# Keys laid out by halves, a result left transposed, and engine orders written group by group

## What is computed

```python
def _cma(x1, x2, ln1_g, ln1_b, ln2_g, ln2_b, Wq, bq, Wk, bk, Wv, bv, Wo, bo):
    x1n, x2n = _ln(x1, ln1_g, ln1_b), _ln(x2, ln2_g, ln2_b)
    q, k, v = x1n @ Wq + bq, x2n @ Wk + bk, x2n @ Wv + bv
    attn = softmax(einsum('bqe,bke->bqk', q, k) * E ** -0.5)
    return einsum('bqk,bke->bqe', attn, v) @ Wo + bo
res = _cma(x, c, ...) + _cma(x, f, ...) + x
x1 = _ln(res, ln_g, ln_b) @ fc_W + fc_b + res
Q, K, V = x1 @ Wq + bq, c @ Wk + bk, c @ Wv + bv
out = x1 + softmax(Q K^T * 128 ** -0.5) V @ Wo + bo
```

## Time and profile before

| what | value |
| --- | --- |
| median of 3 runs | 215.62 us (215.46 to 215.97) |
| the profiled execution | 217.09 us, span 215.3 us |
| mean granted TensorE clock | 0.96 |
| PE busy | 184.8 us (86%) |
| DVE busy | 168.8 us (78%) |
| POOL busy | 148.7 us (69%) |
| ACT busy | 141.8 us (66%) |
| DMA | 22.16 MB, mean 103 GB/s |

### The profile page before, as it was taken

The page is one execution under the profiler, slowest core; times in us unless marked ns, Lnnn a source line. Parts: engine busy times, 40 slices in busy tenths (PEclk is TensorE's granted clock), DMA queues, the critical chain, the costliest instruction groups (busy, mean ns, idle before and its releaser), DMA issues.

```text
span 215.3 us, 6455 instructions
## 1 busy us (share of the span) xinstructions
PE 184.8 (86%) x2380; PEld 138.8 (64%) x2380; DVE 168.8 (78%) x613; ACT 141.8 (66%) x381; POOL 148.7 (69%) x267
## 2 busy tenths in 40 slices
PE   0499687989899999999999999999999999896942
PEld 0386466767676767677776767777676767564531
DVE  5573675888989898989898989899999696966212
ACT  2336681777778787878787877878786866465140
POOL 1878878889797979787878787888788860412000
PEclk9999996999999999999999999999999999998585
DMA  5630441322325151616160807080704050204011
GB/s 148 190 146 2 148 142 59 100 97 95 106 79 169 51 195 30 218 32 218 9 237 6 240 5 232 15 242 9 238 13 146 3 146 3 97 3 146 0 50 52
DMA packets 13570, 22.16 MB, mean 103 GB/s; under 512 B 1825, under 2 KB 4129, under 8 KB 13538
## 3 DMA queue, kind: packets, MB, share of 16 engines
q1 hardware_dynamic: 13538, 21.74, 31.9%
HBM read 17.54 MB, written 4.19 MB: 101 GB/s over the span
## 4 chain that ended last, share of the span: by engine, by line
DVE 44%; PE 29%; ACT 11%; issue 11%; DMA 2%; SPq 1%; DVEq 0%
ACT exp L459 10%; PE ps_s L833 8%; DVE s_m L637 7%; DVE stats L634 6%; DVE out_sb L585 6%; DVE max L620 5%; DVE res_sb L630 5%; DVE sum L570 5%; PE ps_d L734 4%; PE ps_g L819 3%; DVE minus_max L592 2%; DVE rsum L572 2%; DVE s_diff L641 2%; DMA w_sb<-in_w 2%; PE ps_g L745 1%
## 5 line engine op out<-in xcount | busy, mean ns | idle before, releaser
L354 POOL TENSOR_TENSOR rstd<-st_var,minus_half 128x4 f32<-128x4 f32 (+1 forms) x32 | 42.6, 1332 | 2.2
L485 ACT ACTIVATE z_sb<-x_sb,shift,rstd 128x128 f32<-128x128 f32 x64 | 26.4, 485 | 6.8 <-POOL shift L362 6.8
L383 POOL TENSOR_TENSOR resb_sb<-res_sb,row_bias 128x512 f32<-128x512 f32 x16 | 20.4, 1275 | 13.8 <-DVE res_sb L630 13.7
L585 DVE SCALAR_TENSOR_TENSOR out_sb<-ps_g,rsum,x_sb 128x128 f32<-128x128 f32 x64 | 17.9, 343 | 7.7 <-PE ps_g L745 7.7
L387 POOL TENSOR_TENSOR rstd<-s_var,minus_half 128x4 f32<-128x4 f32 x16 | 16.3, 1017 | 10.1 <-DVE s_var L645 10.1
L620 DVE TENSOR_REDUCE max<-ps_s 128x8 f32<-128x512 f32 x16 | 11.1, 692 | 14.0 <-PE ps_s L833 14.0
L459 ACT ACTIVATE exp<-ps_s,minus_max 128x64 f32<-128x64 f32 x64 | 19.2, 312 | 3.5 <-DVE minus_max L592 2.6
L604 DVE SCALAR_TENSOR_TENSOR x_sb<-ps_d,rstd,resb_sb 128x128 f32<-128x128 f32 x64 | 17.9, 342 | 4.4 <-PE ps_d L803 4.4
L516 DVE BATCH_NORM_STATS2 stats<-cf_sb 128x6 f32<-128x64 f32 x128 | 18.7, 212 | 2.1 <-DMA cf_sb<-in_cf 2.1
L494 ACT ACTIVATE t_sb<-ps_d,t_bias 65x512 f32<-65x512 f32 x16 | 10.9, 683 | 12.1 <-PE ps_d L752 12.1
L778 PE MATMUL ps_z<-zT_sb,m 128*128 128x512 f32 x32 | 18.1, 649 | 0.8 <-ACT zT_sb L436 0.8
(11 more groups left out here) (141 smaller groups left out, 460.3 us busy)
## 6 DMA issues: line engine op xcount, KB each, us to landing
cf_sb<-in_cf SPq DMA_DIRECT2D x16, 256.0 KB, 2.6
x_sb<-in_x SPq DMA_DIRECT2D x16, 256.0 KB, 3.0
xres_sb<-in_x SPq DMA_DIRECT2D x16, 256.0 KB, 4.5
out<-out_sb SPq DMA_DIRECT2D x16, 256.0 KB, 4.2
ct_sb<-in_ct SPq DMA_DIRECT2D x16, 128.0 KB, 4.6
c_sb<-in_c SPq DMA_DIRECT2D x16, 128.0 KB, 4.3
w_sb<-in_w SPq DMA_DIRECT2D x1, 384.0 KB
w_score_sb<-in_w_score SPq DMA_DIRECT2D x1, 128.0 KB, 2.3
```

The costliest lines, as they stand in the source:

```text
L354: pool.tensor_tensor(rstd0[:, slot, cols], st_var[:, cols], minus_half[:, cols], ALU.pow).then_inc(st_rstd_done, 1)
L383: pool.tensor_tensor(resb_sb[:, :, :], res_sb[:, slot, :, :], row_bias[:, :].unsqueeze(1).broadcast_to([P, PAIRS, D]), ALU.add).then_inc(r ...
L485: last = nc.scalar.activation(z_sb[:, slot, p, :], x_sb[:, slot, p, :], ACT.Identity, bias=shift0[:, slot, p:p + 1], scale=rstd0[:, slot, ...
L585: last = v.scalar_tensor_tensor(out_sb[:, slot, p, :], ps_g[:, p % 2, (p // 2) * D:(p // 2 + 1) * D], rsum1[:, p:p + 1], x1_sb[:, slot, p, ...
```

## The change

- Keys by halves. cf is laid out in memory by_keys: the partition halves now hold two sequences' keys (v) with c and f side by side, so that c1 is not loaded at all and mix1 reads cf_sb. s0's output has the query's sequence on the partition halves and the source in two banks. s0 and mix1 go through the four corners of the array in the order TILES = (0,0), (1,1), (1,0), (0,1).
- Result transposed. out1 has w1 as its weights and makes the result transposed; the final step is one addition with x1T, and the host transposes. The second softmax is therefore scaled by rsum1 ahead of its transpose (probs1); exp1 is written back into ps_r. row_bias becomes a column that the x1T copy adds, and resb is gone.
- x and cf have a buffer for each group and are loaded once; most intermediates have two buffers or more.
- The banks: ps_s (two) serves cfT, s0, prob1T and mix1; ps_r serves resT and s1.
- The variance of res moves to GpSimd for groups 4 to 12; the power of the statistics is one operation. For groups 0 and 1 VectorE takes the variance and ScalarE normalises cf (early_cfn); ScalarE copies the first folds and issues the first weight loads.
- The step loop is gone: each engine has a list of calls with their groups written out. Each TensorE call also waits until its bank has been read (bank_read).

The diff, cut to its core:

```diff
-LAG_STATS, LAG_NORM, LAG_SCORE, LAG_MIX, LAG_DENSE, LAG_ATT1, LAG_FINAL, LAG_STORE = range(8)
-STEPS = GROUPS + LAG_FINAL
-SLOTS = 2
...
+EARLY = 2
+AHEAD = 4
+X_SLOTS, CT_SLOTS, OUT_SLOTS = GROUPS, 5, 3
+CFN_SLOTS, RES_SLOTS, X1T_SLOTS, RSTD_SLOTS, Z_SLOTS, SLOTS = 4, 4, 4, 4, 3, 2
+VAR1_ON_POOL = range(4, 13)
...
@@ PSUM banks @@
-        ps_z = bank("ps_z", [P, 512])
-        ps_s0 = bank("ps_s0", [P, 512])
-        ps_s1 = bank("ps_s1", [P, 512])
-        ps_d = bank("ps_d", [P, 512])
-        ps_o0 = bank("ps_o0", [P, 512])
-        ps_g = bank("ps_g", [P, 2, 512])
-        ps_g1 = bank("ps_g1", [P, 512])
+        ps_z = bank("ps_z", [P, 512])
+        ps_s = bank("ps_s", [P, 2, 512])
+        ps_r = bank("ps_r", [P, 512])
+        ps_d = bank("ps_d", [P, 512])
+        ps_p = bank("ps_p", [P, 512])
+        ps_g = bank("ps_g", [P, 2, 512])
...
@@ sync @@
-                    need(sp, res_done, g - SLOTS + 1)
-                    sp.dma_start(xres_sb[:, slot, :, :], x[g, :, :, :]).then_inc(xres_in[slot], 16)
-                    sp.dma_start(c1_sb[:, slot, :, :, :], c1[g, :, :, :, :]).then_inc(c1_in[slot], 16)
...
+            load_x(0)
+            load_cf(0)
+            load_x(1)
+            load_cf(1)
+            sp.dma_start(w128_sb[:, :, :], w128).then_inc(late_weights_in, 16)
+            sp.dma_start(wt_sb[:, :, :], wt).then_inc(late_weights_in, 16)
+            sp.dma_start(rows_sb[:, :, :], rows).then_inc(late_weights_in, 16)
+            for g in range(2, GROUPS):
+                if g >= AHEAD:
+                    sp.wait_ge(cf_in[g - AHEAD], 16)
+                load_x(g)
+                load_cf(g)
+                if g - 2 < CT_SLOTS:
+                    load_ct(g - 2)
+            for g in range(GROUPS):
+                if CT_SLOTS + g < GROUPS:
+                    load_ct(CT_SLOTS + g)
+                store(g)
+            for slot in range(OUT_SLOTS):
...
@@ gpsimd @@
-                    need(pool, x1_done, g)
-                    pool.wait_ge(res_done, g + 1)
-                    pool.tensor_tensor(resb_sb[:, :, :], res_sb[:, slot, :, :],
-                                       row_bias[:, :].unsqueeze(1).broadcast_to([P, PAIRS, D]),
-                                       ALU.add).then_inc(resb_done, 1)
...
-                    for half, cols in enumerate((slice(0, PAIRS), slice(PAIRS, 3 * PAIRS))):
...
+                pool.tensor_tensor(rstd0[:, slot, :], st_var[:, g % SLOTS, :], minus_half[:, :],
+                                   ALU.pow).then_inc(rstd0_done, 1)
...
+            def variance_res(g):
+                n, slot = VAR1_ON_POOL.index(g) + 1, g % SLOTS
+                pool.wait_ge(stats1_done, g + 1)
+                pool.tensor_tensor(p1_m2[:, :], stats1[:, slot, :, 2], stats1[:, slot, :, 5], ALU.add)
+                pool.tensor_tensor(p1_diff[:, :], stats1[:, slot, :, 1], stats1[:, slot, :, 4],
...
+            early_rstd_x(0)
+            early_shift_x(0)
+            early_rstd_cf(0)
+            early_shift_cf(0)
+            early_rstd_x(1)
+            early_shift_x(1)
+            early_rstd_cf(1)
+            early_shift_cf(1)
+            variances(2)
...
@@ scalar @@
+            act.dma_start(cols128_sb[:, :], cols128).then_inc(cols_in, 16)
+            act.dma_start(cols64_sb[:, :], cols64).then_inc(cols_in, 16)
+            act.dma_start(w_score_sb[:, :, :], w_score).then_inc(first_weights_in, 16)
+            act.dma_start(w64_sb[:, :, :], w64).then_inc(first_weights_in, 16)
...
+            def early_cfn(g):
+                act.wait_ge(cf_in[g], 16)
+                act.wait_ge(e_cf_shift_done, g + 1)
+                for h in range(2):
+                    for p in range(PAIRS):
+                        at = (1 + h) * PAIRS + p
+                        last = nc.scalar.activation(cfn_sb[:, g, p, h, :], cf_sb[:, g, p, h, :], ACT.Identity,
+                                                    bias=shift0[:, g, at:at + 1], scale=rstd0[:, g, at:at + 1])
+                last.then_inc(e_cfn_done, 1)
...
+                nc.scalar.activation(x1T_sb[:, g % X1T_SLOTS, :], ps_d[:, :], ACT.Identity, bias=row_bias[:, :]
+                                     ).then_inc(x1T_copied, 1)
...
+                    last = nc.scalar.activation(ps_r[:, p * S:(p + 1) * S], ps_r[:, p * S:(p + 1) * S], ACT.Exp,
+                                                bias=minus_max1[:, slot, p:p + 1], accum_out=sum1[:, slot, p:p + 1])
...
+            copy_early_folds_1()
+            z(0)
+            copy_early_folds_2()
+            copy_zT(0)
+            early_cfn(0)
+            copy_t0(0)
+            z(1)
+            copy_cfT(0)
+            copy_late_folds_1()
+            copy_zT(1)
+            early_cfn(1)
+            softmax0(0)
+            copy_t0(1)
+            copy_late_folds_2()
+            copy_cfT(1)
+            z(2)
+            copy_prob0T(0)
+            copy_bq1()
+            copy_zT(2)
+            softmax0(1)
+            copy_mix0(0)
+            copy_t1_bias()
+            copy_cfT(2)
+            copy_t0(2)
+            z(3)
+            copy_prob0T(1)
+            copy_resT(0)
+            softmax0(2)
+            copy_mix0(1)
+            copy_zT(3)
+            z(4)
+            copy_t0(3)
+            copy_cfT(3)
+            copy_x1T(0)
+            copy_zT(4)
+            z(5)
+            copy_t0(4)
+            copy_resT(1)
+            copy_t1(0)
+            softmax0(3)
+            copy_cfT(4)
+            copy_prob0T(2)
+            copy_zT(5)
...
@@ vector @@
-                        last = v.scalar_tensor_tensor(
-                            out_sb[:, slot, p, :], ps_g[:, p % 2, (p // 2) * D:(p // 2 + 1) * D],
-                            rsum1[:, p:p + 1], x1_sb[:, slot, p, :], ALU.mult, ALU.add)
...
+            def probs1(g):
+                dve.wait_ge(rsum1_done, g + 1)
+                need(dve, prob1T_made, g - SLOTS + 1)
+                v.tensor_tensor(prob1[:, g % SLOTS, :, :], by_pair(ps_r[:, 0:PAIRS * S]),
+                                rsum1[:, g % SLOTS, :].unsqueeze(2).broadcast_to([P, PAIRS, S]),
+                                ALU.mult).then_inc(prob1_done, 1)
...
+            def final(g):
+                slot = g % OUT_SLOTS
+                dve.wait_ge(out1_made, g + 1)
+                if g >= OUT_SLOTS:
+                    dve.wait_ge(out_stored[slot], landed(g - OUT_SLOTS, OUT_SLOTS))
+                v.tensor_tensor(out_sb[:, slot, :].rearrange("p (u t) -> p u t", u=DUOS),
+                                ps_g[:, :, 0:2 * P],
+                                x1T_sb[:, g % X1T_SLOTS, :].rearrange("p (u t) -> p u t", u=DUOS),
+                                ALU.add).then_inc(final_done, 1)
...
@@ tensor @@
-                    for p in range(PAIRS):
-                        for b in range(2):
-                            for half in (LOW, HIGH):
-                                last = mm(ps_s0[half, (2 * p + b) * S:(2 * p + b + 1) * S],
-                                          t0_sb[half, p, b, :], cfT_sb[half, p, b, :], start=True, stop=True)
+            def s0(g, sem, count):
+                pe.wait_ge(t0_copied, g + 1)
+                pe.wait_ge(cfT_copied, g + 1)
+                bank_read(sem, count)
+                for u in range(DUOS):
+                    for v in range(2):
+                        p = 2 * u + v
+                        for h, b in TILES:
+                            last = mm(ps_s[HALF[b], h, p * S:(p + 1) * S], t0_sb[HALF[h], g % SLOTS, p, b, :],
+                                      cfT_sb[HALF[h], g % SLOTS, u, b, v, :], start=True, stop=True)
+                last.then_inc(s0_made, 1)
-                        for q in range(DUOS):
-                            for b in range(2):
-                                for half in (LOW, HIGH):
-                                    last = mm(ps_g1[half, (2 * q + b) * S:(2 * q + b + 1) * S],
-                                              c1_sb[half, att1_slot, q, b, :], prob1T_sb[half, q, b, :],
-                                              start=True, stop=True)
+            def mix1(g, sem, count):
+                pe.wait_ge(prob1T_copied, g + 1)
+                bank_read(sem, count)
+                for b in range(2):
+                    for v, u in TILES:
+                        last = mm(ps_s[HALF[u], v, b * S:(b + 1) * S], cf_sb[HALF[v], g, 2 * u + b, 0, :],
+                                  prob1T_sb[HALF[v], g % SLOTS, u, b, :], start=True, stop=True)
+                last.then_inc(mix1_made, 1)
-                        for q in range(DUOS):
-                            for h, half in ((0, LOW), (1, HIGH)):
-                                last = mm(ps_g[:, h, q * D:(q + 1) * D], mix1_sb[half, q, :, :], w1[half, :],
-                                          start=True, stop=True)
+            def out1(g, sem, count):
+                pe.wait_ge(mix1_copied, g + 1)
+                bank_read(sem, count)
```

(165 more changed lines are left out.)

1690 lines of the change are left out of this document (1151 added, 539 removed).

## The result

The changed kernel takes 196.06 us (median of 4, 195.20 to 196.58), the kernel before 215.68 beside it; the ratio is 0.909 (0.904 to 0.913). The forecast was 197. The profiled execution took 196.57 us and has a span of 194.5 us. An execution over 1.5% above the quickest of its kernel is counted as slow, and the medians and ratios here are of the fast ones alone; the profiles of the two-corner run and of the late t0 run are of slow ones, and only their middle is read, where the granted clock is 1.00 as in the changed kernel.

What follows compares the result with a forecast made beforehand. TensorE was taken to set the pace, with VectorE close behind. Start 45.5, middle 130.9 and tail 20.8 sum to a span of 197.2 us, median 197 (191 to 202 at chance 0.56; wider range 188 to 207).

Steps and rivals of the forecast that it cites:

- What bounds: Steady step: TensorE sets the pace, working 10.51 of 11.03 us; faster VectorE alone gives back at most 0.5 us a group.
- a sign of being wrong: Middle of the changed profile: VectorE or ScalarE busy over TensorE would show the forecast wrong.
- the corner argument: s0 and mix1 on TensorE: four array corners, as in mix0, save 0.39 and 0.26 us a group.
- out1 priced at 0.78: out1 on TensorE: two matmuls of 256 columns replace four of 128, adding 0.14 us a group; bounds 0.52 and 1.03.
- The middle, 130.9: From s0 of group 4 to out0 of group 15: 124.8 us of TensorE work at busy share 0.953.
- the share of 0.953: TensorE's busy share of the old steady step, kept for the middle: more slack elsewhere, but one more PSUM user per chain.
- The start, 45.5: Up to s0 of group 4: first product at 7.1, then ScalarE's long list, 36.5 us, sets the time; bounds 42 and 48.
- The tail, 20.8: Behind out0 of group 15: last group's chain 16.0 us plus handoffs, low-clock calls and queueing; bounds 18 and 24.
- Rival 1: Middle: handoffs through the shared bank pair ps_s set the pace, period 11.2 us, 206 us in all; chance 0.12.
- Rival 3: s0 and mix1 keep 1.08 and 0.61 us despite four corners, 8.5 us more, 206 us; chance 0.07.
- Rival 4: The lists fit well: share 0.985, start 42.5, middle 126.7, tail 19.5, 189 us in all; chance 0.14.
- Rival 2: Slower than before: ps_s calls hold TensorE's in-order queue, period past 11.9 us, 224 us at 0.9 a handoff; chance 0.06.

Runs made afterwards that it cites:

- the two-corner run: Changed kernel with s0 and mix1 issuing all products of two opposite array corners first, then those of the other two; median 196.83 us, ratio 0.904.
- the late t0 run: Changed kernel with t0 issued twice for groups 9 to 15; median 200.38 us, ratio 0.923.
- the filled run: Changed kernel with 20 extra TensorE products ahead of the first folds and 4 to 11 in each early gap; 193.42 us, ratio 0.892.

## Why the prediction was right, point by point

- What bounds: TensorE, with VectorE close behind. Right; TensorE's busy share rose from 0.953 to 0.982 in the middle (119.9 of 122.1), and 83 to 90% of late work on TensorE comes through. Not seen: that VectorE is fuller than TensorE from 50 to 70 us (9.86 and 9.72 of 10 against 9.19 and 9.40). The prediction had named that as a sign of being wrong, and for this early part of the middle it was.
- Where the time went, a group: the step of 11.03 us became 122.1/12.5 = 9.8. Of the 1.26 us between, s0 and mix1 are 0.67, TensorE's idle time 0.34 (0.52 before, 2.2/12.5 = 0.18 now), and some 0.25 are closer borders between calls. No run undid the written lists, the second buffers or the lighter work of VectorE, so the 0.34 and the 0.25 are not divided among them.
- s0 priced at 0.69, measured 0.63; mix1 0.35, measured 0.39; the corner argument by mix0's rows held in size. That it would be worth 0.65 us a group: 0.67.
- out1 priced at 0.78, measured 0.63: the term was mis-sized by 0.15 us a group, 1.9 us over the middle. Its bound of 0.52 was the nearer one.
- The middle, 130.9 against 122.1. Two terms were too large: the share of 0.953 kept from before (measured 0.982, worth some 4 us), and the work of a group, 10.0 against 119.9/12.5 = 9.6 (5 us, of which out1 is 1.9; the rest is small overlaps at call borders, as t1 next to t0, 0.91 where it was priced at 1.01). The added user of ps_s cost next to nothing: reads of ps_s ended only 0.33 us of TensorE's gaps over 0.15 us in the middle.
- The start, 45.5 against 52.4. The failing step is "from there ScalarE's written order is long": I let ScalarE work without a gap. It was busy 31.9 us of the 40 between 10 and 50. Of the 8.0 us that it waited between its first fold copy and s0 of group 4, the makers of t0 and zT on TensorE ended 5.2; the longest wait, 2.82 us, was for t0 of group 1, which stood behind s0 of group 0 and folds at the low clock. The first product came at 8.53 and not 7.1, since the weights landed behind the prefetch (6.10 without it). How the 6.9 us divide between the low clock, the first product and plain waiting is not settled, as the filled run has its own delay. The terms 2.76 for eight activations of early_cfn (2.4) and 0.69 for the x1T copy (0.1 added) were sound.
- The tail, 20.8 against 19.9: right. Of the calls priced as slow, the last out1 took 1.23 us; the last t1 took 1.04, so that term was too large.
- VectorE: the result in 0.68 and probs1 in 0.42 as priced, s_m's wait nearly gone. Exp in place takes 0.29, against 0.31: no cost.
- Rival 1 (ps_s sets the pace) is out: TensorE is idle for 0.24 us from 110 to 160 us, and no read of ps_s ended that gap. Rival 3 is out by s0's row. Rival 4 (189) had the better share, 0.985 against 0.982; its middle of 126.7 was still 4.6 us too long and its start of 42.5 was wrong by 10. Rival 2 did not occur.

The right total owes much to luck: the start came out 7 us above the forecast and the middle 9 us below. The start's own upper bound, 48, was passed. The forecast of the span, 197.2, was off by 2.7 us; the median was put only 0.2 us above the span, while it lies 1.6 above the profiled span (the profiled execution itself 2.1), and that brought the two closer.
